# Decoder layer on one core: head loads issued from one queue one at a time, and a bias copy moved behind the mixing loop

## The reference

```python
x = x + _L0_attn_ref(_layernorm(x, axis=-1), Wq, Wk, Wv, lambda_params, g1, g2, g3, W1, W2)
x = x + _L0_xattn_ref(_layernorm(x, axis=-1), ctx_512, ctx_512, xWq, xbq, xWk, xbk, xWv, xbv)
x = x + _L0_ffn_ref(_layernorm(x, axis=-1), wi, bi, wo, bo, lora_A, lora_B, gate_w, gate_b)
```

```python
pQ = jax.nn.elu(Q); pK = jax.nn.elu(K)
Q1, Q2 = jnp.split(pQ, 2, axis=-1); K1, K2 = jnp.split(pK, 2, axis=-1)
kv1 = jnp.einsum('bshe,bshd->bsed', K1, V) * SCALE
kv2 = jnp.einsum('bshe,bshd->bsed', K2, V) * SCALE
w1 = jnp.einsum('bshe,bsed->bshd', Q1, kv1)
w2 = jnp.einsum('bshe,bsed->bshd', Q2, kv2)
attn = w1 - lmb * w2          # then norms, two products with a gelu, residual
```

## Time and profile before

| | us |
|---|---|
| median of 3 runs | 843.0 |
| lowest, highest | 838.57, 844.95 |
| profiled execution, its own time | 842.42 |
| span of that execution in the trace | 840.7 |
| weights and projection | 0 to 130.0 |
| heads | 130.0 to 290.6 |
| 16 products for the bias row | 290.6 to 297.8 |
| mixing, then tail | 298.1 to the end |

### The profile page before, as it was taken

How to read it: one execution, slowest core, us unless ns; L and a number is a source line. 1 busy time by engine, 2 the same in 40 slices (tenths; PEclk the granted TensorE clock), 3 DMA queues, 4 the chain that set the end, 5 groups by cost and what they waited for, 6 DMA issues and landing times.

```text
span 840.7 us, 22097 instructions
## 1 busy us (share of the span) xinstructions
PE 674.5 (80%) x8346; PEld 624.0 (74%) x8346; DVE 496.1 (59%) x1237; ACT 359.3 (43%) x814; POOL 331.8 (39%) x393
## 2 busy tenths in 40 slices
PE   5785896566666725766756899999999999999998
PEld 4564675455555615656644799999999999999998
DVE  4763653222222127787854687777777777777763
ACT  4463661111112215443433454555555555555442
POOL 0131330000000079888814355454455455545323
PEclk9897996555555777677785899999999999999999
DMA  8479687556565212323320001110011110110000
GB/s 256 69 180 205 167 161 175 78 78 104 103 103 128 69 33 100 101 92 107 100 95 19 20 21 32 33 33 18 16 31 31 31 31 31 31 31 12 14 14 26
DMA packets 86567, 62.65 MB, mean 75 GB/s; under 512 B 30680, under 2 KB 83168, under 8 KB 86496
## 3 DMA queue, kind: packets, MB, share of 16 engines
q1 hardware_dynamic: 85536, 58.50, 28.2%
q10 hardware_dynamic: 960, 3.15, 2.2%
HBM read 36.47 MB, written 25.17 MB: 73 GB/s over the span
## 4 chain that ended last, share of the span: by engine, by line
PE 59%; issue 17%; DVE 12%; POOL 5%; DMA 2%; ACT 2%; SPq 1%; DVEq 0%; POOLq 0%; ACTq 0%
PE banks L599 42%; PE banks L710 5%; PE banks L728 4%; PE banks L743 3%; PE banks L652 2%; DMA xin<-in_x_dram 1%; POOL f_hT_lo L1669 1%; DVE m_t L1339 1%; DVE m_at L1332 1%; POOL m_rh L1580 1%; DVE p_st L1233 1%; DVE m_n L1326 1%; DVE p_xn L1246 1%; DMA n_gw<-in_L_ffn_gate_w_dram 1%; PE banks L663 1%
## 5 line engine op out<-in xcount | busy, mean ns | idle before, releaser
L1669 POOL TENSOR_TENSOR f_hT_lo<-f_hs,f_hT_hi 128x512 fp32r<-128x512 f32 x64 | 87.0, 1360 | 103.2 <-ACT f_hT_hi L1167 103.2
L1300 DVE TENSOR_TENSOR h_sm<-banks,blockmask 128x1024 f32<-128x1024 f32 x32 | 37.7, 1220 | 112.7 <-PE banks L710 112.7
L1580 POOL TENSOR_TENSOR m_rh<-m_ms,mhalf 128x32 f32<-128x32 f32 x16 | 88.3, 5522 | 1.3
L1532 DVE SCALAR_TENSOR_TENSOR f_hs<-banks,nbic,f_h 128x256 f32<-128x256 f32 x128 | 54.6, 478 | 43.1 <-PE banks L599 43.1
L1578 POOL TENSOR_SCALAR m_ms<-m_ss 128x32 f32<-128x32 f32 x16 | 5.2, 324 | 180.2 <-DVE m_ss L1320 179.7
L728 PE MATMUL banks<-h_sm,h_v 64*16 64x64 f32 x2048 | 37.1, 301 | 47.9 <-issue 47.9
L599 PE MATMUL banks<-woT_hi,f_hT_lo 128*128 128x256 f32 x256 | 74.5, 291 | 0.2 <-POOL f_hT_lo L1669 0.2
L599 PE MATMUL banks<-f_adT_hi,lbT_lo 128*128 128x256 f32 x256 | 72.9, 285 | 0.1
L599 PE MATMUL banks<-f_xT_lo,wiT_hi 128*128 128x256 f32 x256 | 72.3, 283 | 0.0
L599 PE MATMUL banks<-f_xT_hi,wiT_hi 128*128 128x256 f32 x256 | 72.3, 282 | 0.0
L599 PE MATMUL banks<-f_xT_hi,wiT_lo 128*128 128x256 f32 x256 | 72.3, 282 | 0.0
(11 more groups left out here) (261 smaller groups left out, 2141.6 us busy)
## 6 DMA issues: line engine op xcount, KB each, us to landing
qk_scratch<-p_qk SPq DMA_DIRECT2D x32, 256.0 KB, 2.5
h_qk<-qk_scratch SPq DMA_DIRECT2D x20, 256.0 KB, 8.9
xin<-in_x_dram SPq DMA_DIRECT2D x8, 512.0 KB, 5.0
v_scratch<-p_v SPq DMA_DIRECT2D x16, 256.0 KB, 4.1
h_v<-v_scratch SPq DMA_DIRECT2D x16, 256.0 KB, 8.3
attn_scratch<-h_wn SPq DMA_DIRECT2D x16, 256.0 KB, 5.9
m_w<-attn_scratch SPq DMA_DIRECT2D x16, 256.0 KB, 2.7
m_x<-in_x_dram SPq DMA_DIRECT2D x16, 256.0 KB, 2.8
```

The costliest lines, as they stand in the source:

```text
L1300: dve.tensor_tensor(h_sm[:, r, 2 * s:2 * s + 2], pairs[s][:, :, :], blockmask[:, :].rearrange("p (o n) -> p o n", o=1).broadcast_to([P, 2, ...
L1532: ins = dve.scalar_tensor_tensor(out=f_hs[:, j % 2, c * T:(c + 1) * T], in0=bank[HB[j]][:, c * T:(c + 1) * T], scalar=nbic[:, f:f + 1], in ...
L1580: pool.tensor_tensor(out_ap, tmp, mhalf[:, 0:width], ALU.pow).then_inc(done, 1)
L1669: pool.tensor_tensor(lo, f_hs[:, j % 2], hi.bitcast(F32), ALU.subtract).then_inc(f_hlo, 1)
```

## The change

- All six loads of a unit come from SP, in the order of the four `h_qk` and the two `h_v`, and before each but the first SP waits until the one before has landed (`in_flight` with `MOST = 1`). After the last `h_v` of a unit it waits for that one too.
- ACT issues no DMA.
- ACT's copy of `brow` stands after its mixing loop.

```diff
-        def q_k_tiles(eng, u, which):
-
-            if u.has(2):
-                eng.wait_ge(h_sd, nth(u, ROUNDS, -ROUNDS))
-                apart(eng)
-            eng.wait_ge(p_stored[u.slot], landed(u, 6))
-            apart(eng)
-            for i in which:
-                eng.dma_start(h_qk[32 * i:32 * i + HD, u.slot].rearrange("x (c h) t -> x c (h t)", c=2 * KD),
-                              qk_d[u.index, i].rearrange("c e h t -> e c (h t)")).then_inc(h_qkin[u.slot], 16)
-
...
+            def in_flight(u, n, most):
+
+                past = n - most
+                if past >= ST:
+                    sp.wait_ge(h_vin[u.slot], u.turn * 16 * SETS + 16 * (past - ST + 1))
+                    apart(sp)
+                elif past >= 0:
+                    sp.wait_ge(h_qkin[u.slot], u.turn * 16 * ST + 16 * (past + 1))
+                    apart(sp)
+
+            MOST = 1
+
             def load_qk(u):
-                q_k_tiles(sp, u, range(ST) if isinstance(u.index, int) and u.index < 2 else range(ST // 2))
+                if u.has(2):
+                    sp.wait_ge(h_sd, nth(u, ROUNDS, -ROUNDS))
+                    apart(sp)
+                sp.wait_ge(p_stored[u.slot], landed(u, 6))
+                apart(sp)
+                for i in range(ST):
+                    in_flight(u, i, MOST)
+                    sp.dma_start(h_qk[32 * i:32 * i + HD, u.slot].rearrange("x (c h) t -> x c (h t)", c=2 * KD),
+                                 qk_d[u.index, i].rearrange("c e h t -> e c (h t)")).then_inc(h_qkin[u.slot], 16)
 
             def load_v(u):
                 if u.has(2):
                     sp.wait_ge(h_ed, nth(u, ROUNDS, -ROUNDS))
-                apart(sp)
+                    apart(sp)
                 for c in range(SETS):
+                    in_flight(u, ST + c, MOST)
                     sp.dma_start(h_v[HT * c:HT * c + HT, u.slot].rearrange("p e n -> p (e n)"),
                                  v_d[u.index, TG * c:TG * c + TG].rearrange("t (h e) n -> h t (e n)", e=HD)
                                  ).then_inc(h_vin[u.slot], 16)
+                for n in range(MOST):
+                    in_flight(u, ST + SETS + n, MOST)
...
-            over_units(act, SU, [(2, head_rows(1)), (0, load_q_k), (3, head_natural(2)), (3, head_natural(3)),
+            over_units(act, SU, [(2, head_rows(1)), (3, head_natural(2)), (3, head_natural(3)),
                                  (1, head_rows(0)), (2, head_natural(0)), (2, head_natural(1))])
 
 
-            act.wait_ge(s_brow, 1)
-            act.activation(brow[:, :], bank[7][:, 0:D], ACT.Copy).then_inc(s_browd, 1)
...
+            act.wait_ge(s_brow, 1)
+            act.activation(brow[:, :], bank[7][:, 0:D], ACT.Copy).then_inc(s_browd, 1)
             act.wait_ge(s_w["rows"], 16 * N_ROWS)
```

More of the change, by code:

```diff
@@ L991, in _ @@
             over_units(act, SU, [(2, p_exps(0)), (2, p_exps(1)), (1, p_split), (2, p_exps(2)), (2, p_exps(3)), (2, p_values(0)), (2, p_values(1))])
[L994 to L997, removed]
             def head_rows(r):
```

## The result

| | before | changed |
|---|---|---|
| median, us | 843.98 (4 runs) | 872.84 (4 runs) |
| lowest, highest | 838.57, 848.66 | 870.76, 874.72 |
| profiled execution: time, span | 842.42, 840.7 | 870.76, 869.0 |

The account below looks back on a forecast made before the run. PE was taken as busiest, its instructions delayed by loads under way; serial loads would instead make PE wait for them. Profiled 842.4 + 48.1 (heads end later) - 7.3 (bias copy) = 883 us, range 848 to 908.

Parts of the forecast that it names:

- the sum's five steps: Unit 0's loads, unit 1's loads, units 2 to 7, the end of the heads and the bias copy; total 883 us.
- the end of the heads: From unit 7's last q/k load at 314.6: 11.1 plus 13.0 us, so the heads end at 338.7, 48.1 us later.
- A lone load: Each serial load in the heads: 4.3 us for `h_qk`, 3.3 for `h_v`, 0.12 handling; 24.5 us a unit.
- Times 46: A load and its handling, 4.08 us, count 46 times: all but the first of the first two units.
- Unit 0's loads: In the projection, x of unit 4 lands at 88.7 instead of 74.40 behind these serial loads: +14.3 us.
- Unit 1's loads and the late stores: Loads last until 152.9, then 12 stores take 11 us; SP reaches q and k of unit 2 at 163.9, not 137.41.
- Units 2 to 7: Heads: v of unit 2 at 191.1, units 3 and 4 24.5 us each, then 27.1 each; v of unit 7 at 321.4.
- The bias copy: Start of the mixing: with ACT's copy of `brow` gone from ahead of it, mixing starts 7.3 us sooner: -7.3.
- ACT's issues at nothing: ACT's 12 DMA issues, some 0.4 us each, were beside PE's work, so dropping them counts nothing.
- a lone load is as quick as `m_w`: Rival, faster: heads loads take 2.85 us with handling, heads end 8 us sooner, time 827 us; chance 0.09.
- The fit from the Trainium skill's page "DMA: Bandwidth & Descriptors": About 2.0 us plus bytes over 436 GB/s: 2.6 us for a 256 KB load whatever its partitions.
- the gaps were to be under 2 us: Sign in the changed profile: PE's "issue" gaps in the heads under 2 us, its scores waiting for DMA.

Follow-up runs that it names:

- first_two_free: Changed kernel, but the loads of units 0 and 1 are issued without waits, those of units 2 to 7 one at a time; 850.64 us, ratio 1.009.
- store_first: Changed kernel with the store of the head results ahead of the loads in each of SP's steps; 873.35 us, ratio 1.034.
- copy_alone: The kernel before with only ACT's bias copy moved behind the mixing loop; 836.94 us, ratio 0.994.
- serial_alone: Changed kernel with the bias copy back ahead of the mixing; 880.99 us, ratio 1.044.
- two_in_flight: Changed kernel with up to two loads under way, alternating between two semaphores; 831.16 us, ratio 0.984.
- two_late: Changed kernel with two loads under way, `h_qk` order 0, 2, 1, 3, and loads of units 0 and 1 moved to SP's steps 8 and 9; 822.40 us, ratio 0.975.

## Why the prediction was right

The direction and the mechanism hold, and of the sum's five steps only the end of the heads was incomplete. The size is 10 us too high; against the profiled execution 12 us, of which 9.2 lie before the end of the heads and 3.0 in the later stages, where the change explains nothing. Part of the closeness is luck, since an error of 13.8 us and one of 4.6 the other way met in the sum.

1. *A lone load.* Forecast 4.3 and 3.3 us, measured, in the changed kernel (median us to landing):

```profile
h_qk<-qk_scratch SPq DMA_DIRECT2D x32, 256.0 KB, 4.0
h_v<-v_scratch SPq DMA_DIRECT2D x16, 256.0 KB, 3.3
...
m_w<-attn_scratch SPq DMA_DIRECT2D x16, 256.0 KB, 2.8
```

The same 256 KB take 4.0, 3.3 and 2.8 us to 16, 64 and 128 partitions, the last with a load of `m_x` 0.5 us behind it. My 4.3 us leant on two things. One was 4.6 us for the first of a pair, slower than a lone load. The other was 115 GB/s at full share, read as a stretch with only these loads, though x of unit 4 (62.40) and a store (from 63.12) were issued in it. A unit without store took 23.4 us, 3.89 a load, not 24.5 and 4.08. Times 46 this is 8.7 us: the term that was mis-sized.

2. *Unit 0's loads.* Forecast +14.3 for x of unit 4, measured +11.5. Of the 2.8 us, 1.0 is an earlier start, 1.4 the price of the loads and 0.4 x itself. The stores of unit 2 and x of unit 5 cost nothing, as said: the heads start 10.8 us late, no later than x.
3. *Unit 1's loads and the late stores.* Unit 2's loads were to be issued at 163.9 and went out at 160.5, though the 12 stores took 12.5 us of SP's time and not 11. That this delay counts in full when the loads are serial is shown by first_two_free.
4. *Units 2 to 7.* The last `h_v` was to land at 321.4 and landed at 307.6 (304.20 and 3.36 us). Of the 13.8 us, 3.4 came from step 3, 2.6 from unit 2, 2.1 from units 3 and 4, and 5.7 from the last three, where a store costs 2.0 us and not 2.6.
5. *The end of the heads.* This step was incomplete. I had 24.1 us from unit 7's last `h_qk` to the last `h_wn`; it took 28.7 (300.8 to 329.5). PE waited 6.41 us for ACT's `h_wn`, and ACT for a store that SP's list put behind unit 7's last `h_v`. I had named what is queued behind SP's waits in the projection, but not in the heads. In store_first, where this wait is gone, heads to mixing was 4.2 us shorter in the profile; its median does not show a gain.
6. *The bias copy.* -7.3 forecast; 5.1 (2.9 to 7.2) in copy_alone, 8.2 between serial_alone and the changed kernel.
7. *ACT's issues at nothing.* No run has ACT issuing while loads are serial, so this is not tested; the sum needs nothing more for it. Where no load waits, taking them from ACT cost some 4 us (ratio 0.998 against 0.994; the medians say 6, on two chips).

So the heads' end, forecast 48.1 us later, was 38.9 later (329.5 against 290.6): 13.8 us less up to unit 7's loads, 4.6 us more behind them.

The rival "a lone load is as quick as `m_w`" is refuted by 4.0 against 2.8 us. The fit from the Trainium skill's page "DMA: Bandwidth & Descriptors" that stands beside it is given there for DMAs issued from GpSimd, while these come from SP. Its 2.6 us are 1.4 short of a lone `h_qk`. The rival's other half, that PE gets its instructions sooner, is true, though the gaps were to be under 2 us and the longest was 2.6, and two_in_flight turns it into time. One at a time nearly halves PE's gaps (53.6 to 29.0 us), but the DMA engines' share over the heads falls from 0.52 to 0.37 and PE waits for loads. Two at a time keep only a third of that gain (45.6 us), but the share stays at 0.51 and PE waits for no load.

## What to carry to other kernels

When a queue is made to wait for each transfer, multiply a lone transfer's time from issue to landing by the number on the list, and compare with the pace of the engine that consumes them. If that is too slow, let two be under way before giving the limit up. List everything that stands behind the waiting instruction in each loop it occurs in, stores of results included, and check whose buffer they free. A load that is not needed soon should not stand ahead of one that is on the chain of waits.

## What was not expected of the hardware

- PE's instructions arrive later the more data is queued. The gaps inside groups of equal products were at longest 2.6 us with one 256 KB load under way (3.1 in store_first), 3.6 with two (4.2 in two_late), 7.1 with the mixture before, and 8.31 with ten issued in a row. Where no load was under way a gap was 1.41 us.
- The traces show that these gaps are waits for instructions. In the 5.56 us gap before 161.58 PE has nothing to do from 156.02 on. Between 152.2 and 158.3 us no piece moves on the instruction queue; of 158.3 to 159.9 the profile of the kernel before has:

```profile
q1 hardware_dynamic: 70, 0.23, 111.8%
q8 instruction: 1, 0.02, 5.7%
```

This one piece of 16 KB starts at 158.39 and has landed at 159.84, and PE goes on 1.7 us later. The same holds for 85 of the 86 gaps over 2 us in the heads of the twelve kernels: each ends 1.2 to 2.0 us after such a piece has landed. Before the longest gaps ended, the piece began to move only 1.5 to 5.4 us after PE had stopped. With one load under way it began at most 0.3 us after the stop, or ahead of it. What holds it back, the data ahead of it or something else, no row shows.
- Six loads a unit from SP alone made the kernel some 4 to 6 us slower than four from SP and two from ACT, issued at another time; order and queue were not separated.
